# Second attention: output projection moved into the second pass, part of VectorE's work moved to GpSimd

## The reference

```
x = layernorm(h)                                   # mean and variance of each row of 256
x = (x - mean(x)) / sqrt(var(x) + EPS) * ln_gamma + ln_beta
q, k, v = x @ Wq.T + bq, x @ Wk.T + bk, x @ Wv.T + bv          # 16 heads of 16
s = (q @ k.T) / 4
s = sigmoid(s - mu) * exp(s)
s = s / sum(s)
h = h + (s @ v) @ Wo.T + bo
```

## Time and profile before

| what | value |
|---|---|
| median of 3 runs | 738.07 us (735.27 to 738.28) |
| the profiled execution, own time | 733.83 us |
| its span, first to last instruction | 732.0 us |
| busy in the span: PE, DVE, ACT, POOL | 676.8, 462.8, 344.9, 149.7 us |
| second attention in the trace | about 509 to 700 us |
| starts of pass 2 on ACT, iterations 0 to 7 | 522.64, 547.01, 570.09, 593.16, 616.24, 639.31, 661.65, 682.12 us |

### The profile page before, as it was taken

How to read it: one execution, slowest core, us unless ns; L and a number is a source line. 1 busy time by engine, 2 the same in 40 slices (tenths; PEclk the granted TensorE clock), 3 DMA queues, 4 the chain that set the end, 5 groups by cost and what they waited for, 6 DMA issues and landing times.

```text
span 732.0 us, 15954 instructions
## 1 busy us (share of the span) xinstructions
PE 676.8 (92%) x5553; PEld 540.4 (74%) x5563; DVE 462.8 (63%) x1185; ACT 344.9 (47%) x604; POOL 149.7 (20%) x185
## 2 busy tenths in 40 slices
PE   5799999999989999999999999998899999998855
PEld 4668877877768989877878799997576667765533
DVE  3768787888673362266632332433589999978786
ACT  2354346335534112122222222221898989898745
POOL 3010041232132220000000022600434555211000
PEclk9999999999999999999999999999999999999965
DMA  6777133322538465746466566561432344212003
GB/s 176 230 211 231 47 93 95 101 71 80 147 101 287 155 229 194 257 154 250 132 246 224 180 199 221 174 205 55 118 85 61 88 116 116 72 44 60 1 15 102
DMA packets 70323, 102.85 MB, mean 141 GB/s; under 512 B 8406, under 2 KB 57822, under 8 KB 70118
## 3 DMA queue, kind: packets, MB, share of 16 engines
q1 hardware_dynamic: 66860, 93.46, 40.4%
q0 software_dynamic: 3136, 8.40, 3.7%
q10 hardware_dynamic: 256, 0.07, 0.0%
HBM read 64.41 MB, written 12.19 MB: 105 GB/s over the span
## 4 chain that ended last, share of the span: by engine, by line
PE 68%; DVE 15%; issue 6%; ACT 6%; DMA 3%; POOL 1%; DVEq 1%; SPq 1%; ACTq 0%; POOLq 0%
PE psum L2401 16%; PE psum L2348 14%; DVE arena L1515 4%; PE psum L2292 4%; PE psum L2014 4%; PE psum L2306 4%; PE psum L2277 3%; PE psum L2283 3%; PE psum L2338 2%; DVE arena L1370 2%; PE psum L2038 2%; PE psum L2076 2%; ACT arena L972 1%; DMA arena<-in_L_ffn_w_dram 1%; PE psum L2593 1%
## 5 line engine op out<-in xcount | busy, mean ns | idle before, releaser
L2401 PE MATMUL psum<-arena 128*128 (+1 forms) x576 | 130.7, 380 | 1.9 <-DVE arena L1713 1.4
L2348 PE MATMUL psum<-arena 128*128 128x128 f32 x1024 | 120.5, 276 | 1.4 <-issue 1.0
L2348 PEld LDWEIGHTS psum<-arena 128*128 128x128 f32 x1024 | 118.1, 192 | 4.4 <-issue 3.5
L2401 PEld LDWEIGHTS psum<-arena 128*128 128x128 f32 (+1 forms) x576 | 103.2, 184 | 18.8 <-issue 3.2
L1006 ACT ACTIVATE arena<-psum,arena 128x128 f32<-128x128 f32 x128 | 36.5, 368 | 149.2 <-DVE arena L1687 118.3
L2292 PE MATMUL psum<-arena 99*128 99x256 bf16 (+1 forms) x512 | 73.7, 274 | 5.1 <-ACT arena L971 4.3
L1515 DVE TENSOR_TENSOR arena<-arena 128x1024 f32<-128x1024 f32 x64 | 77.7, 1284 | 0.6 <-ACT arena L971 0.6
L1713 DVE TENSOR_TENSOR arena<-psum,arena 128x256 f32<-128x256 f32 (+1 forms) x40 | 17.0, 424 | 96.5 <-PE psum L2401 81.0
L2292 PEld LDWEIGHTS psum<-arena 99*128 99x128 bf16 (+1 forms) x512 | 44.8, 98 | 35.4 <-ACT arena L971 12.1
L816 POOL DMA_INDIRECT w0T<-yg,pos x32 | 35.3, 1104 | 165.8 <-DMA yg<-arena 157.4
L971 ACT ACTIVATE arena<-psum 128x1024 f32<-128x1024 f32 x64 | 62.0, 1033 | 13.0 <-DVE arena L1713 8.5
(11 more groups left out here) (364 smaller groups left out, 1283.0 us busy)
## 6 DMA issues: line engine op xcount, KB each, us to landing
arena<-in_L_ffn_w_dram SPq DMA_DIRECT2D x48, 1024.0 KB, 5.2
arena<-arena SPq DMA_DIRECT2D x192, 128.0 KB, 2.4
yg<-arena SPq DMA_DIRECT2D x36, 128.0 KB, 1.8
arena<-xg SPq DMA_DIRECT2D x32, 128.0 KB, 2.3
out_dram<-arena SPq DMA_DIRECT2D x8, 256.0 KB, 2.1
xg<-zeros SPq DMA_DIRECT2D x9, 128.0 KB, 2.8
arena<-in_x_dram SPq DMA_DIRECT2D x8, 128.0 KB, 2.3
arena<-in_L_ffn_b_dram SPq DMA_DIRECT2D x1, 1024.0 KB, 13.9
```

Source lines behind the costliest of these rows:

```text
L2348: mm = pe.matmul(psum[:, 2 * v + c // HALF, (c % HALF) * P:(c % HALF + 1) * P], w1[:, d, c * P:(c + 1) * P], xtT[:, v, d, :], start=(d == ...
L2401: mm = pe.matmul(y_bank[0:rows], hidT[:, u, c, 0:rows], w2s[:, one(e), c, :].rearrange("p o n -> p (o n)"), start=(c == 0), stop=(c == HC ...
```

## The change

The change moves work in the second attention on three engines, and ACT's and SP's lists stay as they are.

- DVE gives up `norm1` of batches 2 to 7 and `split_last` of batches 1 to 7. POOL does both: it has a `norm1` of its own behind `scale1`, and `last_part` behind each `second_part`. DVE's two waits before `split_rest` are now for the last parts.
- On DVE `sum_h3` and `stat2` move from the place before `biased_v` to the place between product 2 and product 3.
- On PE the two projection tiles of batch b - 1 move from behind `pass1(6)` and `pass1(7)` to behind `pass2(2)` and `pass2(3)`, where they replace two of the three pairs of idle products, the four products of the title. In iteration 0 the idle products at these two places go without a replacement.

```diff
@@ gpsimd
+                def norm1(b):
+                    wait(pool, S["n_xT_mm"], b)
+                    pool.wait_ge(S["n_rstd"], b + 1)
+                    for q in range(QT):
+                        pool.tensor_scalar(n_xh[:, q, :], h[:, b * QT + q, :], n_mom[:, 0, q, 0:1],
+                                           n_rs[:, 0, q:q + 1], ALU.subtract, ALU.mult).then_inc(S["n_xh"], 1)
...
+                def last_part(b, which, middle, done):
+                    pool.wait_ge(middle, b + 1)
+                    pool.tensor_tensor(n_qkp[which][:, 2], n_qkr[which], n_qkp[which][:, 1], ALU.subtract).then_inc(done, 1)
...
                     if stages(b + 2, 3, LAST):
                         scale1(b + 2, 0, S["n_mv"], S["n_rstd"])
+                        norm1(b + 2)
                     if stages(b + 1, 1, LAST):
                         second_part(b + 1, 0, S["n_qr"], S["n_qm"])
+                        last_part(b + 1, 0, S["n_qm"], S["n_ql"])
                         second_part(b + 1, 1, S["n_kr"], S["n_km"])
+                        last_part(b + 1, 1, S["n_km"], S["n_kl"])
...
                 gather(3)
+                norm1(2)
                 all_batches(iteration)
@@ vector
-                        wait(dve, S["n_qm"], b + 1)
+                        wait(dve, S["n_ql"], b + 1)
                         split_rest(b + 1, 0, S["n_qh"], S["n_qr"])
                     if stages(b - 2, 0, LAST):
                         maximum(b - 2)
                     if stages(b + 1, 0, LAST):
-                        split_last(b + 1, 0, S["n_qm"], S["n_ql"])
-                    if stages(b + 1, 0, LAST):
-                        wait(dve, S["n_km"], b + 1)
+                        wait(dve, S["n_kl"], b + 1)
                         split_rest(b + 1, 1, S["n_kh"], S["n_kr"])
-                    if stages(b + 2, 3, LAST):
-                        norm1(b + 2)
-                    if stages(b + 1, 0, LAST):
-                        split_last(b + 1, 1, S["n_km"], S["n_kl"])
-                    if stages(b - 1, 0, LAST):
-                        sum_h3(b - 1)
-                    if stages(b - 1, 0, LAST):
-                        stat2(b - 1)
                     if stages(b + 1, 1, LAST):
                         biased_v(b + 1, v)
                     for p in range(PAIRS):
                         if stages(b, 0, LAST):
                             multiply(b, u, p)
-                        if b == 0 and p == 2:
-                            norm1(2)
+                        if p == 2 and stages(b - 1, 0, LAST):
+                            sum_h3(b - 1)
+                            stat2(b - 1)
@@ tensor
                     pass1(6)
-                    if stages(b - 1, 0, LAST):
-                        pe.wait_ge(S["n_oT"], b)
-                        project_token_tile(misc[0], n_oT, 3, 0)
                     pass1(7)
-                    if stages(b - 1, 0, LAST):
-                        project_token_tile(misc[0], n_oT, 3, 1).then_inc(S["n_wo"], 1)
...
                     pass2(2)
-                    idle_products(2)
+                    if stages(b - 1, 0, LAST):
+                        pe.wait_ge(S["n_oT"], b)
+                        project_token_tile(misc[0], n_oT, 3, 0)
                     pass2(3)
-                    idle_products(2)
+                    if stages(b - 1, 0, LAST):
+                        project_token_tile(misc[0], n_oT, 3, 1).then_inc(S["n_wo"], 1)
```

## The result

The changed kernel takes **746.25 us** (median of 4 runs, 742.6 to 746.99). The kernel before, run beside it, takes 736.67 (734.37 to 738.28). The ratio is 1.0121, with a 95% interval of 1.0083 to 1.0160: slower by 9.6 us, where 745.9 and +7.8 were predicted.

The account below looks back on a forecast made before the run. The prediction took a ring with DVE's products on the path as the bound: +3.0 for iterations 1 to 4, +1.5, +1.7, +2.0 and -0.4 make +7.8 on 738.07, so 745.9 us, range 740.5 to 752.

Parts of the forecast that it names:

- Sum and statistics, +2.0: On DVE between products 2 and 3: they come onto the path and cost 2.0 us per iteration, 1 to 7.
- one-input statistics are not lengthened beside `biased_h`: On DVE beside POOL: statistics reading one SBUF input are lengthened by 0, with 1.4 as the other end.
- The stall, -1.08: Iterations 1 to 4: POOL's new work delays `biased_h`, so it no longer holds product 2, gaining 1.08 us each.
- The rival that the stall stays: `biased_h` meets product 3 or 4, so 1.08 isn't given back in four iterations: +4.3, 750.2; chance 0.11.
- Product 0, -0.18: Iterations 1 to 4: with normalisation and last parts off DVE, product 0 starts earlier after pass 2, gaining 0.18 us.
- Iterations 5 and 6: No stall to give back; the sum's +2.0 less an earlier product 0 and some slack: +1.5 and +1.7 us.
- Iteration 7: Product 0 already starts as early as it can, and the last product begins the attention's tail: +2.0 us.
- the clock: Rival: PE's clock falls on `values`, up to 1.8 us less 0.18 each; three falls give 750.7; chance 0.05.
- Iteration 0: No sum in it; `norm1` leaves the products, `values` waits less, `biased_h` is pushed into product 0: -0.4 us.
- Tiles in pass 2, 0: On PE: the projection tiles cost 0, hidden by product 3's delay; without it, 0.6 less the 0.51 PE waited.
- The markers: Signs of being right: no product above 1.3 us, `biased_h` beside the sum, PE's group 1 and ACT waiting over 1.
- The base: The time the sum was added to: 738.07 us, the median of the runs, 4.24 above the profiled execution.

Follow-up runs that it names:

- `proj_back`: The changed kernel with the projection tiles back behind `pass1(6)` and `pass1(7)` and the idle products back in pass 2; 746.65 us, ratio to before 1.0149.
- `pool_only`: POOL's part of the change alone, with sum, statistics and tiles where the kernel before had them; 736.81 us, ratio 1.0012.
- `stats_twice`: The changed kernel with the two `bn_stats` of `stat2` done twice, the first into a tile nothing reads; 749.11 us, ratio 1.0177.
- `sum_last`: The changed kernel with `biased_h` ahead of POOL's gathers and with sum and statistics behind product 7; 740.05 us, ratio 1.0061.
- `no_pool`: The kernel before with sum, statistics and tiles moved, while DVE keeps its normalisation and last parts; 748.38 us, ratio 1.0159.
- `bias_first`: The kernel before with POOL's `biased_h` put ahead of the four gathers, nothing else; 733.08 us, ratio 0.9962.

## Why the prediction was right, and where it was not

**Sum and statistics, +2.0: right.** Product 3 starts 1.84 after product 2's end, on a pitch that had let them overlap by 0.08: 1.92. `proj_back` beside `pool_only` shows its price alone, `stats_twice` and `sum_last` show it from both sides. That one-input statistics are not lengthened beside `biased_h` held: 0.75 for the pair at 579.50, beside POOL's 1.29 from 579.56, and 0.75 in iteration 7 with nothing on POOL. The Trainium skill (SBUF — State Buffer, Who interferes with whom) has a VectorE instruction outside the two-port modes contend with GpSimd only when it has two SBUF inputs and the GpSimd instruction reads SBUF, and the port pair that they share is an exclusive lock; the trace agrees, with the 0.75 here and with the product held for 1.08 under `biased_h`.

**The stall, -1.08: right in kind, 0.18 short.** `biased_h` came 5.4 after pass 2, not 4.5, so it ran past the statistics and cost product 3 0.18 in iterations 1 to 4. Two terms of POOL were mis-sized. The gathers start 1.45 later against pass 2, where I had 1.2; and from the first gather to `biased_h` they take 6.51 instead of 5.87, a term I had taken as fixed. The third and fourth gather, now beside products, take 1.56 and 1.96 where they took 0.95 and 1.51, and the first 1.08 where it took 1.51 beside a last part; that DVE's work makes them longer fits this, but no run separates it. The last parts were shorter than I thought (1.16), and the normalisation (2.44), which I hadn't priced, lay almost wholly in time in which POOL had waited for DVE. The rival that the stall stays was nearer than its 0.11 suggests: about 1 us more on POOL, and `biased_h` would have started together with product 3.

**Product 0, -0.18: right in size, put under the wrong part.** It starts 1.05 or 1.06 after pass 2 in all eight iterations. I had booked it under the normalisation and the last parts off DVE. But `no_pool`, with these on DVE, has 1.06, and `proj_back` and `pool_only`, without them and with the tiles at their old place, have 1.23. So it is the tiles' leaving PE ahead of `values` that gains it, and relieving DVE gains nothing.

With these, iterations 1 to 4 come out: 1.92 - 1.08 - 0.18 + 0.18 = +0.84.

**The rows of before, read too coarsely.** ACT idles five times in iteration 2 after the products have begun, not three: the earlier trace rows leaves out 0.26 before 582.84 and 0.47 before 586.05, both for PE. And the 0.32 before group 3 in the earlier trace rows is idle time of the weight loads; PE's own matmuls pause only 0.07 there. So in iteration 2 it is product 3 that holds PE first, and product 7 adds only 0.07 to that; the change moves the ends of both by the same 0.84. The terms of the forecast do not hang on either reading.

**Iterations 5 and 6: right** (+1.38 and +1.57 for +1.5 and +1.7): no stall to give back, so they pay nearly the whole sum.

**Iteration 7: the term was 0.8 too small.** 1.9 is the sum, as predicted; 0.88 is the half clock. I had named the clock as a rival, but at `values`, with 0.05; it fell on the tiles instead. `values` ran at full clock in iteration 0. That is hardly a matter of the execution alone: the three kernels in which DVE keeps the normalisation (before, `no_pool`, `bias_first`) all have a stretch at half clock there, from 521.8 to 522.9 on, and product 0 starts 2.96 to 3.05 after pass 2; the eight others have full clock at `values` and product 0 at 1.06. In the three, PE waits 0.27 to 0.36 for DVE ahead of `values`, in the others it doesn't. The rival had the change bring the clock down at this place; instead the half clock went away with POOL's part. Whether PE's wait had brought it, no run shows.

**Iteration 0: right by two errors.** The sum of -0.4 stands against -0.29, but product 0 starts 1.06 after pass 2 instead of 2.96 (-1.9: the half clock of the earlier trace rows is not there, and `values` is no longer late), and the products take 11.43 instead of 9.81 (+1.6). DVE and POOL:

```profile
527.24 11.43 DVE L1532 TENSOR_TENSOR arena<-arena 128x1024 f32<-128x1024 f32 x8 [0.16 <-ACT arena L989]
```

```profile
527.67 2.01 POOL L844 TENSOR_TENSOR arena<-arena 128x512 bf16<-128x512 f32 x1
529.65 2.26 POOL L825 TENSOR_TENSOR h<-h,bo 128x512 f32<-128x512 f32 x1
```

A cast of POOL (526.98, 0.61 us), its last part and `biased_h` lie beside the first three products here, which take 1.43, 2.17 and 2.30. The last part and `biased_h` are held too (2.01 and 2.26 us instead of 1.16 and 1.29).

**Tiles in pass 2, 0: right for this kernel only.** Beside the sum they are hidden (`proj_back`). Without it I had reckoned 0.6 less the 0.51 that PE waited, so 0.1; `sum_last` shows 0.59, since PE, which does the tiles, has become the path there: all of the 0.59 arises on PE ahead of group 0.

**The markers.** Product 3 takes 1.38 to 1.41 in iterations 1 to 4, so "no product above 1.3" failed, and `biased_h` lies beside the statistics and not the sum. PE's group 1 waits 0.76 for DVE and not over 1; ACT idles 0.68 before `pass1(0)` and not over 1, because the tiles had already let it wait 0.93 within pass 2. By my own figure for the seventh and eighth function I should have expected that.

**The base.** I put the sum on the median of the runs shown. It landed at 745.9 against 746.25 with +7.8 instead of +9.6, because the runs of before beside the changed kernel had a median 1.4 lower. A match to 0.4 us is thus partly luck; the periods are the better test.

## What to carry to other kernels

Look at what ends last in one iteration, and price a move by what then stands on that path, not by the engine that is relieved: 2 us that had hidden in a wait cost 2 us between the products, while four instructions taken out of the same engine's slack gained nothing. Where two engines hold each other, try the order first: one instruction moved ahead of the gathers on POOL gave 0.4% (0.2% by the medians), where the larger change cost 1.2%. Follow each gain to the next bound (22.35 here), and keep the ends of a pipeline apart from its middle: what is hidden in the middle is paid for in the last iteration.

## What the runs showed of the hardware

- The normalisation of 128 x 256 takes POOL 1.22 us (2.44 the pair); on DVE the pair had taken 1.02 in iteration 2. A last part (two inputs, 128 x 512) takes POOL 1.16, and DVE 0.69 when undisturbed.
- `biased_h` (1.3 to 1.4 us) cost the DVE instruction that it met 1.07 or 1.08 us: product 2 before, product 4 in `pool_only`, a last part in `bias_first`. In these it held one instruction and never two, though the products follow each other without a pause.
- The granted clock fell to 1.2 GHz for stretches of 3.4 to 13.7 us, in the first 31 us and in the last iteration at places that differ between executions of nearly the same program; in the second attention one such stretch of 3.4 us cost the last iteration 0.88. At `values` of iteration 0 it fell in three of three kernels in which DVE keeps the normalisation and in none of eight others.
